# Attention part of a fused block: chunks taken in sets of three instead of pairs

## The reference

```
x = x + attention(gn(x), registers, qkv_w, qkv_b, out_w, out_b)
x = x + experts(gn(x), router_w, router_b, fc1_w, fc1_b, fc2_w, fc2_b)

attention: q, k, v = heads(x @ qkv_w.T + qkv_b);  reg_k, reg_v from the registers
  scores = einsum('bnqe,bnke->bnqk', q, [k, reg_k]) / sqrt(32)
  scores = where(7x7 window or register, scores, -1e30)
  out    = (softmax(scores) @ [v, reg_v]) @ out_w.T + out_b
```

## Time and profile before

| | us |
|---|---|
| median of three runs | 647.62 |
| lowest, highest | 646.08, 648.91 |
| span of the profiled execution | 648.7 |
| TensorE busy (matmul) | 570.3 (88%) |
| VectorE busy | 447.4 (69%) |
| ScalarE busy | 308.6 (48%) |
| GpSimd busy | 294.5 (45%) |
| maxima, 216 instructions of line 558 | 108.2 |
| exponentials, line 885 | 78.6 for 162 of the 216 |

### The profile page before, as it was taken

How to read it: one execution, slowest core, us unless ns; L and a number is a source line. 1 busy time by engine, 2 the same in 40 slices (tenths; PEclk the granted TensorE clock), 3 DMA queues, 4 the chain that set the end, 5 groups by cost and what they waited for, 6 DMA issues and landing times.

```text
span 648.7 us, 22391 instructions
## 1 busy us (share of the span) xinstructions
PE 570.3 (88%) x9227; PEld 399.9 (62%) x9227; DVE 447.4 (69%) x1009; ACT 308.6 (48%) x609; POOL 294.5 (45%) x433
## 2 busy tenths in 40 slices
PE   3578779999899988998999988898887889998998
PEld 2336666667665866667776776655765656665554
DVE  6885575777887777775667777876688796873333
ACT  1762455215634298512663145451588337754221
POOL 3116699155222667435993362223757232313131
PEclk8799999999999998998999999899998899999999
DMA  9769674995339952397527955179651002121213
GB/s 305 181 153 287 170 203 142 222 282 152 102 77 238 242 150 67 86 261 210 154 59 172 270 170 158 33 181 264 178 141 46 3 0 74 39 74 37 74 37 109
DMA packets 130636, 94.10 MB, mean 145 GB/s; under 512 B 67132, under 2 KB 124392, under 8 KB 130536
## 3 DMA queue, kind: packets, MB, share of 16 engines
q1 hardware_dynamic: 121032, 73.85, 43.4%
q0 software_dynamic: 9504, 18.84, 9.4%
HBM read 56.29 MB, written 35.54 MB: 142 GB/s over the span
## 4 chain that ended last, share of the span: by engine, by line
PE 63%; DVE 12%; ACT 6%; issue 6%; DMA 5%; SPq 4%; POOL 3%; POOLq 0%; ACTq 0%; DVEq 0%
PE ps L1065 44%; PE ps L1229 6%; PE ps L1180 5%; PE ps L1206 4%; SPq L267 3%; DVE ST L450 2%; ACT PT L885 2%; DVE MX L558 2%; DMA QS<-MT 2%; DMA KB<-kscr 1%; ACT XH L826 1%; DMA X<-in_x 1%; SPq L250 1%; POOL vscr L361 1%; POOL X L390 1%
## 5 line engine op out<-in xcount | busy, mean ns | idle before, releaser
L558 DVE TENSOR_REDUCE MX<-ps 128x2 f32<-128x372 f32 x216 | 108.2, 540 | 65.9 <-PE ps L1180 65.2
L1065 PE MATMUL ps<-XH,WQ 128*128 128x384 f16 x810 | 142.1, 330 | 8.6 <-DVE XH L499 7.7
L1065 PEld LDWEIGHTS ps<-XH,WQ 128*128 128x128 f16 x810 | 78.0, 99 | 63.6 <-ACT XH L826 7.6
L885 ACT ACTIVATE PT<-ps 128x448 f32<-128x448 f32 (+1 forms) x162 | 78.6, 511 | 40.1 <-PE ps L1206 39.9
L1206 PE MATMUL ps<-QS,KB 122*128 122x112 f16 (+1 forms) x864 | 65.3, 215 | 18.2 <-ACT PT L885 11.9
L430 POOL TENSOR_TENSOR KT<-QS,KT 128x384 f16<-128x384 f32 x36 | 34.3, 963 | 97.2 <-ACT KT L978 97.2
L1180 PE MATMUL ps<-KB,QS 120*32 120x186 f16 x1728 | 57.4, 250 | 17.7 <-issue 6.9
L1206 PEld LDWEIGHTS ps<-QS,KB 122*128 122x128 f16 x864 | 44.1, 100 | 39.5 <-ACT PT L885 20.7
L1065 PE MATMUL ps<-WQ,XH 128*128 128x128 f16 x972 | 62.5, 223 | 4.5 <-issue 4.2
L1065 PEld LDWEIGHTS ps<-WQ,XH 128*128 128x128 f16 x972 | 56.3, 100 | 10.3 <-issue 8.1
L1229 PE MATMUL ps<-PT,VR 128*32 128x112 f32 (+1 forms) x1296 | 61.2, 263 | 1.1 <-DMA VR<-vscr 0.6
(11 more groups left out here) (168 smaller groups left out, 1005.5 us busy)
## 6 DMA issues: line engine op xcount, KB each, us to landing
KB<-kscr SPq DMA_DIRECT2D x108, 192.0 KB, 4.6
kscr<-KT SPq DMA_DIRECT2D x72, 192.0 KB, 2.5
VR<-vscr SPq DMA_DIRECT2D x216, 56.0 KB
QS<-qscr SPq DMA_DIRECT2D x108, 96.0 KB, 5.8
out<-X SPq DMA_DIRECT2D x11, 576.0 KB, 3.3
X<-in_x SPq DMA_DIRECT2D x6, 576.0 KB, 7.3
qscr<-QT POOLq DMA_DIRECT2D x18, 192.0 KB, 3.1
qscr<-PT POOLq DMA_DIRECT2D x18, 192.0 KB, 5.0
```

Source lines behind the costliest of these rows:

```text
L558: V.tensor_reduce(out=MX[:, s % 2, t, 2 * pair:2 * pair + 2], in_=ps[:, S_BANK(s, i), 0:2 * RUN].rearrange("p (h n) -> p h n", h=2), op=AL ...
L885: A(PTS[n % 4][:, 0:w], ps[:, ST_BANK(n), 0:w], ACT.Exp, scale=SCORE).then_inc(s_["exd"], 1)
L1065: last = mm(bank, lhsT(a, k), rhs(b, k), start=(k == 0 and n == 0), stop=(finish and k == steps - 1 and n == 2))
```

## The change

TensorE's list now takes three chunks at a time: key scores of n, n+1, n+2, then the weighted sums of n-3, n-2, n-1. For this the transposed scores get a third bank (6), the sums of all tiles go to bank 7 alone, with a new semaphore `sumt` that is raised when they have been turned, and two more buffers for exponentials lie in the values' buffers, which are laid together in one tensor VW. The maxima are turned behind the key scores of a set; those of tiles 4 and 5 are turned one set later than before, at the head of tiles 3 and 4, and ScalarE copies them out behind the third exponential there. A weight (fc1) is loaded into KT instead of WR.

```diff
-        ST_BANK = lambda n: 2 + n % 2
+        ST_BANK = lambda n: (2, 3, 6)[n % 3]
         O_BANK = lambda s: 4 + s % 2
-        SUM_BANK = lambda s: 6 + s % 2
+        SUM_BANK = 7
...
-        def score_units(s, pair):
+        def score_units(s, part):
             if s == 0:
-                return [(3, pair)]
+                return [(3, 2 * part), (3, 2 * part + 1)]
             if s == 1:
-                return [[(3, 3), (3, 4)], [(3, 5)], []][pair]
-            if s in (2, 3) and pair < 2:
-                return [(s + 2, 3 * pair + i) for i in range(3)]
+                return [(3, 4), (3, 5)] if part == 0 else []
+            if s in (2, 3):
+                return [(s + 2, 3 * part + i) for i in range(3)]
             return []
...
 GpSimd (maxima_in) and ScalarE (maxima_out), in the loops over s and a:
-                        if a == 1 and s == 0:
-                            maxima_out(gi, 2)
-                        if a == 5 and s in (1, 2, 3):
-                            maxima_out(gi, s + 2)
+                        if a == 2 and s in (0, 3, 4):
+                            maxima_out(gi, s + (1 if s else 2))
+                        if a == 5 and s == 1:
+                            maxima_out(gi, 3)
...
 VectorE:
             def reciprocals(gi, s):
                 dve.wait_ge(s_["pv"], 36 * gi + 6 * (s + 1))
-                link(V.transpose(SUMT[:, :], ps[:, SUM_BANK(s), 0:SN]))
+                V.transpose(SUMT[:, :], ps[:, SUM_BANK, 0:SN]).then_inc(s_["sumt"], 1)
+                dve.wait_ge(s_["sumt"], 6 * gi + s + 1)
...
-                        if a == (3 if s in (2, 3) else 1) and s:
+                        if a == 1 and s:
                             reciprocals(gi, s - 1)
-                        if a == 2 and s in (1, 2, 3):
+                        if a == (1 if s == 1 else 3) and s in (1, 2, 3):
                             split_maxima(gi, s + 2)
...
 ScalarE (exps):
-                if 36 * gi + n - 3 > 0:
-                    act.wait_ge(s_["pv"], 36 * gi + n - 3)
+                if 36 * gi + n - 5 > 0:
+                    act.wait_ge(s_["pv"], 36 * gi + n - 5)
...
 TensorE:
-                    pe.wait_ge(s_["exd"], 36 * gi + n - 1)
+                    pe.wait_ge(s_["exd"], 36 * gi + n - 2)
...
+                    if s >= 1:
+                        pe.wait_ge(s_["sumt"], 6 * gi + s)
...
+                for n in range(0, 6 * TILES, SET):
+                    s, part = n // 6, n % 6 // SET
+                    for i in range(SET):
+                        key_scores(gi, n + i)
+                    turned = {(0, 0): 2, (1, 1): 3, (3, 0): 4, (4, 0): 5}.get((s, part))
+                    if turned:
+                        maxima_turned(gi, turned)
+                    units = score_units(s, part)
+                    for unit in units[0:2]:
+                        scores(gi, *unit)
+                    if n:
+                        weighted(gi, n - 3)
+                        weighted(gi, n - 2)
+                    for unit in units[2:]:
+                        scores(gi, *unit)
+                    if n:
+                        weighted(gi, n - 1)
```

More of the change, by code:

```diff
@@ L75, in build @@
         GM = sb("GM", [GROUPS, 2])
-        WR = sb("WR", [P, KC, C])
         ID16 = sb("ID16", [P, P], F16)
@@ L111, in build @@
         PICK = extra[:, 64 + C:64 + 2 * C]
-        wr_flat = WR[:, :, :].rearrange("p k n -> p (k n)")
         ktf = KT[:, :, :, :, :].rearrange("p a b s n -> p (a b s n)").bitcast(F32)
+        f1raw = ktf[:, 0:KC * C]
         f2raw = ktf[:, 0:KC * C]
         rwraw = ktf[:, KC * C:KC * C + KC * EXPERTS]
-        VTS = [VT[:, i, :, :] for i in (0, 1)] + [WR[:, i, :].rearrange("p (b n) -> p b n", n=P) for i in range(3)]
-        b2raw = VT[:, :, :, :].rearrange("p a b n -> p (a b n)")[:, 0:C]
+        VTS = [VW[:, i, :, :] for i in range(5)]
+        b2raw = vw_flat[:, 0:C]
         HW = KT[:, :, :, :, :].rearrange("p a b s n -> p (a b s n)").rearrange("p (a s k n) -> p a s k n", a=2, s=2, k=KC)
@@ L202, in OP_BANK @@
             return (6, 2, 3, 4, 0, 1, 6, 7)[q] if q < 8 else (5, 6, 7)[(q - 8) % 3]
[L204 removed]
+        ST_BANK = lambda n: (2, 3, 6)[n % 3]
         O_BANK = lambda s: 4 + s % 2
[L206 removed]
+        SUM_BANK = 7
         S_BANK = lambda s, i: (6, 5, 7, 0, 1, 4)[i] if s < 3 else (i + 1) % 2
[L208 removed]
+        PW = HEADS * 14 * CT_
+        PTS = [PT[:, i, :] for i in range(3)] + [QT[:, :, :, :].rearrange("p a b n -> p (a b n)").bitcast(F32)[:, 0:PW]] + [
+            vw_flat[:, C + i * PW:C + (i + 1) * PW] for i in range(2)]
+        SET = 3
         T_BANK = lambda s: 6 if s < 2 else 0
[L212 removed]
+        def score_units(s, part):
             if s == 0:
[L214 removed]
+                return [(3, 2 * part), (3, 2 * part + 1)]
             if s == 1:
[L216 to L218 removed]
+                return [(3, 4), (3, 5)] if part == 0 else []
+            if s in (2, 3):
+                return [(s + 2, 3 * part + i) for i in range(3)]
             return []
@@ L286, in _ @@
                     if gi == 4 and s == 2:
-                        for i in (2, 3, 4):
-                            sp.wait_ge(v_out[i], 48 * (gi + 1))
-                        sp.dma_start(wr_flat, fc1).then_inc(s_["f_in"], 16)
+                        sp.dma_start(f1raw, fc1).then_inc(s_["f_in"], 16)
                     if s < 2:
@@ L649, in _ @@
                     for a in range(STRIPS):
-                        if a % 2 == 0:
-                            for unit in score_units(s, a // 2):
+                        if a % SET == 0:
+                            for unit in score_units(s, a // SET):
                                 maximum(gi, *unit)
-                        if a == (3 if s in (2, 3) else 1) and s:
+                        if a == 1 and s:
                             reciprocals(gi, s - 1)
-                        if a == 2 and s in (1, 2, 3):
+                        if a == (1 if s == 1 else 3) and s in (1, 2, 3):
                             split_maxima(gi, s + 2)
@@ L1225, in weighted @@
                 w = CT_ * (q1 - q0)
-                for bank, sums in ((O_BANK(s), False), (SUM_BANK(s), True)):
+                for bank, sums in ((O_BANK(s), False), (SUM_BANK, True)):
                     for h in range(HEADS):
                         lhsT = ONE[:, :] if sums else VR[:, s % 2, a, DH * h:DH * (h + 1)]
-                        last = mm(ps[DH * h:DH * (h + 1), bank, CT_ * q0:CT_ * q1], lhsT, PTS[n % 4][:, h * w:(h + 1) * w],
+                        last = mm(ps[DH * h:DH * (h + 1), bank, CT_ * q0:CT_ * q1], lhsT, PTS[n % 6][:, h * w:(h + 1) * w],
                                   start=(a == 0), stop=(a == STRIPS - 1), skip_group_check=True)
@@ L1291, in _ @@
                         all_values(k)
[L1292 to L1307, removed]
-                        if pair == 0 and s == 0:
-                            maxima_turned(gi, 2)
-                weighted(gi, 34)
-                weighted(gi, 35)
+                for n in range(0, 6 * TILES, SET):
[15 more added lines that the diff above has]
+                        weighted(gi, n - 1)
+                for i in range(SET):
+                    weighted(gi, 6 * TILES - SET + i)
             def logits(img, blk):
```

25 lines of the change are left out of this document (16 added, 9 removed).

## The result

The change makes the kernel slower. Four runs of the changed kernel gave a median of 669.6 us (668.1 to 671.7), four of the kernel before, on the same chip, 648.3 us (646.1 to 651.0); the ratio is 1.034, 95% interval 1.029 to 1.039. The forecast was 665 us, range 649 to 675. The span of the profiled execution is 669.8 us.

The account below looks back on a forecast made before the run. It took ScalarE to bound stages 2 and 5, and a chain of TensorE, VectorE, ScalarE and two DMA queues the others. Stage losses of 16.0 us plus 1.5 for clock, on 647.6, gave 665 us, range 649 to 675.

Parts of the forecast that it names:

- Head of tile 0: Stage 1: unit 1 of tile 3 waits for the copy of tile 2's maxima until 152.6; TensorE stands 1.1 us.
- Middle of tile 1: Stage 1: tile 3's turn waits until about 159.6, tile 4's units start at 161.8 instead of 160.1; hidden by late keys.
- Head of tile 3: Stage 1: tile 5's second unit waits for tile 4's copy, behind rounding and three exponentials: 170.0 instead of 167.4, 2.6 us.
- Head of tile 4: Stage 1: tile 5's maxima, copied late, land at 181.2 instead of 176.15; TensorE stands 1.9 us before its key scores.
- The other stages: Same steps outside stage 1: stage 0 +2.3, stage 2 +2.5, stage 3 +3.3, stage 4 +1.6, stage 5 +2.4 us.
- The clock: Matmuls at 1.2 GHz after TensorE stands, in the attention parts: 1.5 us lost, bounds 0 and 5.4.
- The single sum bank: At tile changes TensorE may wait for the turning of sums: taken as nothing, bounds 0 and 18 us.
- Rival A: The change works as pipelining: copies come in time and waits for exponentials go; 640 us, chance 0.08.
- B: Copy waits happen, but late keys and values cover them and tile 5 catches up; 648 us, chance 0.08.
- C: Only one of the two copy waits holds, as when VectorE gets through earlier; 655 us, chance 0.17.
- both terms: The two deciding waits in stage 1, at the heads of tiles 3 and 4: 2.6 us and 1.9 us.
- D: The forecast's waits, plus the sum bank and a slower clock in all stages; 26 us, 674 us, chance 0.17.

Follow-up runs that it names:

- e1: Changed kernel with ScalarE's copies and GpSimd's sends of tiles 4 and 5's maxima back at the end of tiles 2 and 3: 646.0 us, ratio 1.000.
- e3: Kernel before (pairs, two banks), tiles 4 and 5's maxima turned behind tiles 3 and 4's first key scores, copied and sent one exponential later: 662.9 us.
- e8: e2 with tile 2's turn and copy first, and output rounding after the second exponential of the tile after next: 643.1 us, ratio 0.993 to before.
- e2: e1 with TensorE's turns of tiles 3, 4 and 5 back behind the last weighted sums of tiles 1, 2 and 3: 644.5 us, ratio 0.988.
- e5: Changed kernel with only tile 4's copy and sending of maxima back at the old place: 657.2 us, ratio 1.017 to the kernel before.
- e6: Changed kernel with only tile 5's copy and sending of maxima back at the old place: 665.3 us, ratio 1.028 to the kernel before.
- e11: Kernel before (pairs, two banks) with output rounding after the second exponential of the tile after next, and tile 2's turn and copy first: 639.7 us.

## Why the prediction was right, and where it was not

**Direction and cause** were right. The loss is the two copies behind the rounding and three exponentials; e1 takes it all back and e3 makes most of it alone. Of the signs named, TensorE's second unit of tile 5 waits 2.15 us for MT in stage 1 and 1.92 in stage 3, just under the 2 us asked for; tile 5's key scores wait 1.56 to 2.58 us for the DMA in every part; the rounding waits for ON; and the waits for exponentials are 5.0 us, less than 8.

**Head of tile 0:** forecast 1.1 us of standing and the unit at 152.6, which is 156.8 on the new clock; measured 1.14 us and 156.77.

**Middle of tile 1:** the turn was to come at 159.6 (163.8) after 1.5 us, hidden by the keys for tile 5's units. Measured 163.49 after 1.30 us, and the units still waited 0.36 us for the keys. Hidden, with little to spare.

**Head of tile 3:** forecast 170.0 (174.2), measured 173.63, so the term was 2.0 us and not 2.6. The scaling came earlier than counted: the rounding started at 171.51.

**Head of tile 4:** forecast landing at 181.2 (185.4) with TensorE standing 1.9 us; measured a start at 185.78 after 1.56 us. The part was to be 35.6 us long from the first key score to the end and was 36.4.

**The other stages:** forecast against measured change of the parts' length, before the clock: stage 0 +2.3 / +5.8, stage 1 +3.9 / +4.6, stage 2 +2.5 / +4.0, stage 3 +3.3 / +7.8, stage 4 +1.6 / +1.8, stage 5 +2.4 / +6.1, in sum 16.0 / 30.1. "Stages 1 and 3 must take about 35 us" held for stage 1 (36.4) and not for stage 3 (39.2). There, 11.0 us later on the new clock, the unit started at 338.41 against a forecast of 337.4, and tile 5's key scores at 351.75 against a landing forecast for 349.0; the mean granted clock was 0.57 from 338.4 to 342.4. For stage 2 the working shown gives 260 - 257.97 = 2.0 us, and not the 2.5 in the sum.

**The clock** is the step that failed in size. I had priced it at 1.5 us, with 5.4 as the upper bound. The mean granted clock was 1.00, 1.00, 0.95, 1.00, 0.95, 0.96 in the six parts before and 0.87, 0.95, 0.92, 0.91, 1.00, 0.85 after. I had allowed for one slow stretch in each part at most, as the old profile had it in three parts. The rows say more: length times what the mean lacks to 1.00, doubled, gives by my estimate 10.5 us at 1.2 GHz in the six parts before, 11.0 in e1 and 41 in the changed kernel. In stage 1 it shows in the rows above: after the stand of 2.15 us the 12 wide key scores at 175.46 take 1.22 us, where the 12 wide ones at 167.24 had taken 0.72. The stretches around 175.46 and 179.00, with the granted clock third from the end (0.50 is 1.2 GHz, 1.00 is 2.4):

```profile
175.40:176.70 1.30, 1.30 (x20) 1.11 (x20) 0.95 (x3) 0.64 (x2) 0.00 (x0) 0.50 0.02 2
178.90:180.00 1.10, 1.08 (x30) 0.82 (x25) 1.03 (x4) 0.00 (x0) 0.00 (x0) 1.00 0.27 73
```

A long row alone is no sign of it: the 12 wide key scores at 181.74 take 1.20 us at a clock of 1.00, while ScalarE works off the exponentials that free their banks.

e1 has the same matmuls in the same order as the changed kernel, and a clock of 0.95 or 1.00 in each part; TensorE is busy for 173.0 us there and for 183.3 in the changed kernel. The 10.3 us between them is what the slower clock cost in TensorE's own work, as far as busy times tell it; 30 us more at half speed can hold up to 15 us of lost work, so the size fits. (The kernel before is no measure for this: at nearly the same clock as e1 its pairs show 180.5 us busy.) By stages these are 2.9, 1.1, 0.9, 3.3, -1.2 and 3.2 us, largest in stages 0, 3 and 5, where the forecast fell short most. Put in place of the 1.5, the sum is 16.0 + 10.3 = 26.3 against the 30.1 measured; 3.8 us over six parts stay unexplained. That each us of slower matmuls lengthens its part by a us is argued here and not shown. e3 agrees in direction: 188.5 us busy in its parts against 180.5 before, with 230.6 us of length. The page "TensorE: Matmul & The Clock Gate" of the Trainium skill, section "HAM oscillation — how this bites in real kernels", had said that waits between groups of matmuls cost more than themselves; I let three parts of the old profile speak against it, and it was the better guide here. Yet not every stand lowered the clock: stage 4 has stands of 1.14, 1.36, 1.16 and 2.26 us and a clock of 1.00 throughout. I had said that the new stands lie in every stage, but not counted that each would have three to five of over 1 us, with a slow stretch behind several of them.

**The single sum bank** at nothing was right for this change: one wait of 0.3 us, where 18 had been the bound. It is not nothing once other waits are gone: 2.5 us in e8.

**Rival A** had its mechanism half right. The waits for exponentials did fall, to 5.0 us, below the 8 that I had named. But they were worth little: with all copies in place (e2) they are 9.2 us and the kernel gained 0.5 to 2%, and the pairs with a better order gain as much. The Trainium skill's page "Perfetto Trace Analysis", section "Identifying Performance Opportunities", names too little buffer space as a possible cause of consistent bubbles; the bubbles here shrank with more buffers, so it can name a cause of the bubbles, but the time hardly moved, so it was not what set the time. **B** (late, but covered) fell: nothing covered it. **C** fell as well: both terms held, and e5 and e6 show that each costs 11 us or more by itself. **D** had the clock right in kind (slower in all stages, which holds for five of the six) and its 26 us lie near the 30.1 of the parts, but by a clock twice as costly as its 5.4 us and without the sum bank.

Still open: how the loss divides between the rounding and the exponentials ahead of the copies, why what lies outside the parts differs by up to 9 us between profiles (scatter, or time given back there when the parts are long), whether the two late copies overlap (the medians say so; the parts' lengths, 222.7 us in e5 and 227.7 in e6 against 209.5 and 240.6, nearly add), and whether e11 is faster than e8.

## What to carry to other kernels

When a pipeline is deepened, look first at the small operations that are threaded between the large ones. Here two copies of 0.45 us, moved behind one rounding and three exponentials on an engine that works strictly in order, cost 3.4%, and what the deeper pipeline was made for was worth nothing that could be measured beside the better order in pairs. Read for each of them what stands ahead of it in its queue, what that waits for, and how many instructions stand behind the one that needs it; and don't price a wait at its length alone where TensorE's granted clock falls after it.

## What the runs showed of the hardware

The price of a stand of TensorE. Between e1 and the changed kernel its matmuls are the same and their busy time differs by 10.3 us, a third of the 31.1 us by which the parts differ (240.6 against 209.5). I had expected a tenth. With tile 4's copy late alone (e6) the busy time is 7.1 us above e1's, with tile 5's late alone (e5) 0.8, though the waits that each adds are about the same, 15.7 and 15.0 us. Stands of up to 2.26 us passed in stage 4 of the changed kernel at a granted clock of 1.00.
